# Attention's head on one core: the first unit's transfers split twelve to four between two queues, in place of eight to eight

## The chip, the cores and the metric

The kernel runs on one core of a Trainium2 chip. The time is the device time of one execution in microseconds. Before the change the median of three runs is 663.71 us (662.4 to 664.31).

## The reference

The input x is 4096 tokens of 128 numbers. Three blocks change it in turn, each with a residual:

```python
x = x + 0.5 * ffn(layernorm(x))      # 8 experts, top 2, hidden 176, and a shared expert
x = x + attn(layernorm(x))           # over 4096 fixed memory keys and values, one head of 128
x = x + 0.5 * ffn(layernorm(x))      # the same weights as the first
```

The attention is `softmax((x Wq + bq) K^T / sqrt(128)) V`, then `Wo` and `bo`. Only its output is kept; the update of the memory is not computed.

## The kernel before

The tokens are 8 groups of 512. The first block handles a group at a time (`ffn(0)`), then the attention, then the second block (`ffn(1)`). Each engine has a program of its own written out by hand, and semaphores are the only ties between them. An instruction stands behind all that is before it on its engine.

**The attention is cut in 16 units.** A unit is one group of 512 queries (four tiles of 128) against one half of the keys, 2048 of them. A unit has 8 steps, `h` = 0 to 7: two for each tile `i`, one for each 1024 of the keys. In a step:

- TensorE makes the scores of 128 queries by 1024 keys: six matmuls of 512 columns (`scores`, lines 1311 to 1313), in one of three pairs of PSUM banks. A pair is taken again once the exponential that reads it is done.
- VectorE takes the maximum (line 1061), and after a tile's second one the negative maximum (line 1067).
- ScalarE takes the exponentials (`exponentials`, lines 726 and 736).

For the product with the values the exponentials have to be transposed. There are two ways. Of **moved** tiles (tiles 0 and 1 in the first unit, 0 to 2 in the later ones) VectorE transposes squares of 32 by 32 (`transpose_squares`, line 1056), and DMA transfers put the strips in place (`move_strip`, line 331). Of the **own** tiles (2 and 3 in the first unit) TensorE transposes blocks of 128 into the bank `TB` (`transpose_pair`, line 1331).

**Rings.** The transposed exponentials of a unit are used in eight pieces, the rings. ScalarE rounds each into `p_hi`, with `moved_high` (line 708) for the moved tiles and `own_high` (line 700) for the own ones. GpSimd subtracts for `p_lo` of the moved (`moved_low`, line 513), VectorE for that of the own (`own_low`, line 1049). TensorE multiplies with the values (`values`, lines 1352 to 1354). There is only one bank `TB`, so `transpose_pair` of a ring waits until `own_low` of the ring before is done (line 1323). The order of ScalarE's program around the head is:

1. unit 0, step 5: the sixth exponential; then the waits of lines 789 to 791, then the transfers of lines 792 to 794;
2. step 6: the seventh exponential, then `moved_high` of ring 0, which first waits for all 256 counts of the semaphore `moved[0]`: sixteen transfers of 16;
3. step 7: `own_high` of ring 0, the eighth exponential, `moved_high` of ring 1.

TensorE's program has, at the first step of unit 1, scores, and the transposes of ring 0, which wait for the seventh exponential. At the second step it has scores, and the transposes of ring 1. The third has scores (they wait for the eighth exponential), the values of ring 0, the transposes of ring 2.

VectorE's program has `own_low` of ring 0 ahead of the maximum of the second step of unit 1. From there on every step of TensorE is one group of transposes, six matmuls of scores and six of values.

**The transfers of the first unit.** The two moved tiles are cut in 4 strips of 32 partitions (`i`), and each strip in 4 by the block `b` of queries within the tile: sixteen transfers of 128 KB. They can go once VectorE's four transposes of squares are done. SP issues those with `b` = 0 and 1 (lines 382 to 384), ScalarE those with `b` = 2 and 3. In the later units SP issues sixteen of 128 KB and twelve of 64 KB, and ScalarE four of 64 KB.

SP's program has nothing between the first unit's transfers and those of the second. They wait for squares of the second unit.

Of the kernel before, what the change touches and what calls it, by code (L numbers as in the profile page):

```python
# [45 lines left out]
QUADS = P // SQ  # L46
# [41 lines left out]
def macaron_kernel(nc: bass.Bass, x, wup, wdown, gate_w, expert_bias, shared_up, shared_down,  # L88
                   wq, bq, wo, bo, keys_values, out):
    with ExitStack() as ctx:  # L90
# [170 lines left out]
        def wait(eng, s, n):  # L261

            if not isinstance(n, int) or n > 0:
                eng.wait_ge(s, n)
# [21 lines left out]
        def early_logits(i):  # L286

            return (TB, banks[:, 3, :], banks[:, 1, :])[i][:, 0:GT * E]

        def moved_tiles(w):  # L290

            return 2 if w in (0, LAST) else MOVED
# [27 lines left out]
        def squares_of(units):  # L320
            return 2 * sum(moved_tiles(w) for w in range(units))
# [4 lines left out]
        def move_strip(eng, u, k, b, i):  # L326

            first, count = BATCHES[k]
            target = probsT[b * SQ:(b + 1) * SQ, u % 2, :, :, :].rearrange(
                "p (t i) c q -> p i t (c q)", t=MOVED)[:, i, first:first + count, :]  # L330
            eng.dma_start(target, E2[i * SQ:(i + 1) * SQ, first:first + count, b, :]).then_inc(moved[k], 16)
# [7 lines left out]
        def pair_at(H):  # L339

            return pairs_until(H) if pairs_until(H + 1) > pairs_until(H) else None

        def projection_at(H):

            w = H // HALVES - 2
            if w < 0 or w >= LAST:
                return None
            return w if H % HALVES == (FIRST_LAG if w == 0 else LAG) + 1 else None

        def tiles_of(g):  # L350
            return bass.ds(g * GT, GT)

        @block.sync
        def _(sp):
            sp.dma_start(X[:, 0:GT, :], x[:, 0:GT, :]).then_inc(x_loaded[0], 16)
            sp.dma_start(wup_f, wup).then_inc(up_w_loaded, 16)
            sp.dma_start(X[:, GT:2 * GT, :], x[:, GT:2 * GT, :]).then_inc(x_loaded[1], 16)
            small = [(sup_s[:, :, :], shared_up), (sdown_s[:, :, :], shared_down), (wq_s[:, :], wq), (bq_s[:, :], bq)]
            for dst, src in small:
                sp.dma_start(dst, src).then_inc(small_w_loaded, 16)  # L360
            sp.dma_start(X[:, 2 * GT:3 * GT, :], x[:, 2 * GT:3 * GT, :]).then_inc(x_loaded[2], 16)
            sp.dma_start(wdown_f, wdown).then_inc(down_w_loaded, 16)
            sp.dma_start(X[:, AHEAD * GT:, :], x[:, AHEAD * GT:, :]).then_inc(x_loaded[AHEAD], 16)
            for b in range(2):
                sp.dma_start(kv_stage[:, b, :], keys_values[:, b, :]).then_inc(kv_loaded[b % 2], 16)
            for dst, src in [(wo_s[:, :], wo), (bo_s[:, :], bo.to_broadcast([P, D]))]:
                sp.dma_start(dst, src).then_inc(out_w_loaded, 16)
            for b in range(2, KV):
                sp.wait_ge(kv_lo_done, b - 1)
                sp.dma_start(kv_stage[:, b % 2, :], keys_values[:, b, :]).then_inc(kv_loaded[b % 2], 16)  # L370

            for u in range(UNITS):
                if u == 0:
                    sp.wait_ge(z_done, GROUPS)
                    sp.wait_ge(down_done, GROUPS * SLOTS)
                wait(sp, moved_lo_done, UP * (u - 1))
                for k, (first, count) in enumerate(BATCHES):
                    if first >= moved_tiles(u):
                        continue
                    sp.wait_ge(squares_done, squares_of(u) + 2 * (first + count))  # L380

                    for b in range(QUADS // 2 if u == 0 else QUADS - k):
                        for i in range(QUADS):
                            move_strip(sp, u, k, b, i)
            for g in range(GROUPS):
                sp.wait_ge(x_updated, GROUPS + g + 1)
                sp.dma_start(out[:, tiles_of(g), :], X[:, tiles_of(g), :]).then_inc(stored, 16)
            sp.wait_ge(stored, 16 * GROUPS)
# [179 lines left out]
        def _(act):  # L568
# [25 lines left out]
            def exp_logits(G, logits):  # L594

                act.wait_ge(logits_done, G + 1)
                if G >= 2:
                    act.wait_ge(route_step, STEPS * route_event(G - 2) + 1)
                act.activation(expz[:, G % 2, :, :].rearrange("p t e -> p (t e)"), logits, ACT.Exp, scale=-1.0
                               ).then_inc(expz_done, 1)  # L600
# [16 lines left out]
            def copy_wbc(G, bank):  # L617
                act.wait_ge(wbc_done, G + 1)
                wait(act, weighted, (G - 1) * SLOTS)
                act.activation(wbc[:, G % 2, :], bank, ACT.Copy).then_inc(wbc_copied, 1)  # L620
# [66 lines left out]
            def early_copy(i, bank):  # L687

                if i == 0:
                    act.wait_ge(q_projected, GROUPS)  # L690
                else:
                    act.wait_ge(probsT_done, UP * LAST)
                act.wait_ge(xT_done, SECOND_LN + i + 1)
                act.activation(xT[i], bank, ACT.Copy).then_inc(xT_copied, 1)
# [46 lines left out]
            def copy_oT(w):  # L741

                act.wait_ge(pv_done, (w + 1) * KC)
                wait(act, out_proj_done, w)
                act.activation(oT[:, :], OB, ACT.Copy).then_inc(oT_copied, 1)
# [17 lines left out]
            for u in range(UNITS + 2):  # L763
                g = u // 2
                prepares = u % 2 == 1 and u < LAST
                for h in range(HALVES):
                    H = u * HALVES + h
                    w = projection_at(H + 3)
                    if w is not None:
                        copy_oT(w)  # L770
                    if u == LAST + 2 and h == LAG - 2:
                        copy_oT(LAST)
                    if u == LAST + 1 and h == 3:
                        early_copy(1, banks[:, 1, :])
                    if u == LAST + 1 and h == 5:
                        exp_logits(GROUPS + 1, early_logits(1))
                        early_copy(2, banks[:, 0, :])
                    if u == LAST + 1 and h == 7:
                        exp_logits(GROUPS + 2, early_logits(2))
                    if u == LAST + 2 and h == 3:  # L780
                        copy_wbc(GROUPS, banks[:, 2, :])

                    ring = pair_at(H + 3)
                    if ring is not None:
                        own_high(ring)
                    if u < UNITS:
                        exponentials(u, h // 2, h % 2)
                    if u == 0 and h == 5:
                        act.wait_ge(z_done, GROUPS)
                        act.wait_ge(down_done, GROUPS * SLOTS)  # L790
                        act.wait_ge(squares_done, squares_of(1))
                        for b in range(QUADS // 2, QUADS):
                            for i in range(QUADS):
                                move_strip(act, 0, 0, b, i)
                    if 0 < u < LAST and h == HALVES - 1:
                        wait(act, moved_lo_done, UP * (u - 1))
                        act.wait_ge(squares_done, squares_of(u) + 2 * MOVED)
                        for i in range(QUADS):
                            move_strip(act, u, 1, QUADS - 1, i)
                    if prepares and h == Q_HALF - 2:  # L800
                        copy_xT_for_q(g + 1, TB)
                    if prepares and h == Q_HALF - 1:
                        q_high(g + 1, TB)
                    if u == LAST and h == Q_HALF - 2:
                        early_copy(0, TB)
                    if u == LAST and h == Q_HALF - 1:
                        exp_logits(GROUPS, early_logits(0))
                    ring = pair_at(H + 4)
                    if ring is not None:
                        moved_high(ring)  # L810
                    w = projection_at(H + 2)
                    if w is not None:
                        copy_y(w)
                    if 2 <= u and u % 2 == 0 and h == 1:
                        shift_exponentials(g - 1)
# [668 lines left out]
```

## Time and profile before

| what | value |
|---|---|
| median of three runs | 663.71 us |
| the profiled execution, its own time | 662.44 us |
| its span, first to last instruction | 660.8 us |
| around the span | 1.6 us |
| mean granted TensorE clock | 0.984 of full |
| VectorE busy | 524.5 us (79%) |
| ScalarE busy | 461.3 us (70%) |
| GpSimd busy | 390.0 us (59%) |

Times inside the kernel are counted from the start of the span. The attention's head lies from 113 us on, the first unit's transfers from 130.7. A busy time of TensorE includes the pipelined ends of matmuls, so neighbouring rows overlap. "PEclk" is the granted clock: 1.00 is 2.4 GHz and 0.50 is 1.2 GHz. In the chain of work that ended last an entry "ACTq" is time in which ScalarE's queue issues a transfer. The issue of transfers is not counted as busy.

### The profile page before, as it was taken

How to read it: one execution, taken by the hardware profiler on the slowest of the kernel's cores; microseconds unless marked ns; L12 is line 12 of the kernel's file. 1: busy time of each engine (PE TensorE's matmuls, PEld its weight loads, DVE VectorE, ACT ScalarE, POOL GpSimd, SP SyncE). 2: the span in 40 equal slices, each digit the busy share in tenths (PEclk: the TensorE clock that was granted, in tenths of full speed). 3: DMA queues.
4: the chain of work that ended last, by engine and by line, in shares of the span. 5: the costliest groups of instructions: out<-in, count | busy, mean ns of one | idle time of the engine just before them, and what ended most of it. 6: DMA issues, size and time to landing. Idle time of an engine off the chain costs nothing.

```text
span 660.8 us, 9207 instructions
## 1 busy us (share of the span) xinstructions
PE 614.2 (93%) x2800; PEld 429.1 (65%) x2800; DVE 524.5 (79%) x943; ACT 461.3 (70%) x765; POOL 390.0 (59%) x427
## 2 busy tenths in 40 slices
PE   3899999669899999999999999999999988999997
PEld 2555434447677877777778777777777867645442
DVE  4788877758978888887797897887898957698785
ACT  3567888446668767777776777777776774668886
POOL 3876970025366867767687587696677786524000
PEclk9799999979999999999999999999999998999999
DMA  8012020052573553744735627437355350000000
GB/s 301 1 33 65 32 64 0 2 126 65 128 160 87 137 132 76 172 95 101 160 84 141 135 64 176 107 93 163 90 131 116 84 121 1 0 18 17 32 33 32
DMA packets 35555, 59.06 MB, mean 89 GB/s; under 512 B 8539, under 2 KB 9139, under 8 KB 35379
## 3 DMA queue, kind: packets, MB, share of 16 engines
q1 hardware_dynamic: 31891, 53.75, 33.4%
q10 hardware_dynamic: 3616, 4.73, 2.8%
q8 instruction: 23, 0.38, 0.3%
q14 instruction: 25, 0.20, 0.1%
HBM read 8.12 MB, written 2.10 MB: 15 GB/s over the span
## 4 chain that ended last, share of the span: by engine, by line
PE 67%; DVE 18%; issue 5%; ACT 5%; SPq 1%; POOL 1%; ACTq 1%; DMA 1%; DVEq 0%; POOLq 0%
PE banks L1311 7%; PE banks L1352 7%; PE banks L1353 7%; PE banks L1354 7%; PE banks L1313 7%; PE banks L1312 7%; PE banks L1331 5%; DVE bank_max L1061 4%; DVE E L1056 4%; PE banks L1195 4%; PE banks L1186 3%; PE banks L1202 3%; PE banks L1149 3%; DVE probsT L958 3%; PE banks L1362 2%
## 5 line engine op out<-in xcount | busy, mean ns | idle before, releaser
L513 POOL TENSOR_TENSOR p_lo<-probsT,p_hi 128x768 fp32r<-128x768 f32 (+1 forms) x128 | 226.8, 1775 | 161.9 <-ACT p_hi L708 161.1
L1061 DVE TENSOR_REDUCE bank_max<-banks 128x1 f32<-128x1024 f32 x128 | 156.1, 1220 | 34.8 <-PE banks L1313 33.7
L708 ACT ACTIVATE p_hi<-probsT 128x768 fp32r<-128x768 f32 (+1 forms) x128 | 104.5, 816 | 28.0 <-PE banks L1354 24.0
L1311 PE MATMUL banks<-kv_lo,q_parts 128*128 128x512 f32 x256 | 112.0, 437 | 6.9 <-ACT E L726 4.4
L958 DVE SCALAR_TENSOR_TENSOR probsT<-banks,E 128x1024 bf16<-128x1024 f32 x80 | 95.5, 1218 | 28.7 <-PE banks L1186 28.1
L1056 DVE STREAM_TRANSPOSE E<-E 128x1024 f32<-128x1024 f32 x92 | 113.5, 1234 | 1.7 <-ACT E L726 1.7
L726 ACT ACTIVATE E<-banks,neg_max 128x1024 f32<-128x1024 f32 x92 | 102.3, 1113 | 8.5 <-DVE neg_max L1067 5.3
L1352 PE MATMUL banks<-p_hi,kv_lo 128*128 128x512 f32 x256 | 108.1, 422 | 0.0
L615 ACT ACTIVATE probsT<-probsT 128x1024 bf16<-128x1024 bf16 x96 | 91.8, 981 | 18.7 <-DVE probsT L958 15.5
L1353 PE MATMUL banks<-p_lo,kv_hi 128*128 128x512 f32 x256 | 102.8, 401 | 0.0
L1354 PE MATMUL banks<-p_hi,kv_hi 128*128 128x512 f32 x256 | 102.6, 401 | 0.0
L1313 PE MATMUL banks<-kv_hi,q_parts 128*128 128x512 f32 x256 | 101.6, 397 | 0.0
L1312 PE MATMUL banks<-kv_hi,q_parts 128*128 128x512 f32 x256 | 101.5, 397 | 0.0
L700 ACT ACTIVATE p_hi<-banks 128x256 fp32r<-128x256 f32 (+1 forms) x128 | 52.3, 408 | 63.1 <-PE banks L1331 62.9
L1049 DVE TENSOR_TENSOR p_lo<-banks,p_hi 128x256 fp32r<-128x256 f32 (+1 forms) x128 | 56.1, 438 | 43.1 <-ACT p_hi L700 42.6
L1331 PE MATMUL banks<-ident,probs 128*128 128x128 f32 x272 | 53.5, 280 | 10.7 <-ACT probs L736 6.6
L1311 PEld LDWEIGHTS banks<-kv_lo,q_parts 128*128 128x128 f32 x256 | 48.6, 190 | 15.3 <-ACT E L726 5.8
L1331 PEld LDWEIGHTS banks<-ident,probs 128*128 128x128 f32 x272 | 36.9, 143 | 32.9 <-ACT probs L736 7.0
L1354 PEld LDWEIGHTS banks<-p_hi,kv_hi 128*128 128x128 f32 x256 | 48.4, 189 | 12.4
L1352 PEld LDWEIGHTS banks<-p_hi,kv_lo 128*128 128x128 f32 x256 | 48.5, 190 | 11.8 <-issue 1.7
L1353 PEld LDWEIGHTS banks<-p_lo,kv_hi 128*128 128x128 f32 x256 | 48.5, 190 | 11.7 <-issue 1.7
L1186 PE MATMUL banks<-E,wup_b 128*128 128x512 bf16 x176 | 53.6, 392 | 2.4 <-DVE q_parts L1018 1.1
(118 smaller groups left out, 886.3 us busy)
## 6 DMA issues: line engine op xcount, KB each, us to landing
probsT<-E SPq DMA_DIRECT2D x248, 128.0 KB, 2.4
probsT<-E SPq DMA_DIRECT2D x168, 64.0 KB, 2.0
E<-in_keys_values SPq DMA_DIRECT2D x8, 512.0 KB, 3.5
probsT<-E ACTq DMA_DIRECT2D x56, 64.0 KB, 2.3
out<-X SPq DMA_DIRECT2D x8, 256.0 KB, 2.0
X<-in_x SPq DMA_DIRECT2D x1, 1280.0 KB, 8.9
probsT<-E ACTq DMA_DIRECT2D x8, 128.0 KB, 4.1
X<-in_x SPq DMA_DIRECT2D x3, 256.0 KB, 5.1
```

Source lines behind the costliest of these rows:

```text
L513: pool.tensor_tensor(moved_part(p_lo, ring), moved_pair(ring // UP, ring % UP), moved_part(p_hi, ring).bitcast(fp32), ALU.subtract).then_i ...
L708: act.activation(moved_part(p_hi, ring), moved_pair(ring // UP, ring % UP), ACT.Copy).then_inc(moved_hi_done, 1)
L958: dve.scalar_tensor_tensor(hidden[:, k, :, :], up_banks[PAIR_BANK[k]], 0.0, spread.unsqueeze(1).to_broadcast([P, 2, N]), ALU.max, ALU.mult ...
L1056: dve.transpose(half, half).then_inc(squares_done, 1)
L1061: dve.tensor_reduce(bank_max[:, i % 2, h:h + 1], score_pair(u, i, h).rearrange("p b n -> p (b n)"), AX.X, ALU.max).then_inc(bank_max_done, 1)
L1311: pe.matmul(bank, qh, kl, start=True, stop=False)
L1312: pe.matmul(bank, ql, kh, start=False, stop=False)
L1313: pe.matmul(bank, qh, kh, start=False, stop=True).then_inc(scores_done, 1)
L1331: last = pe.transpose(TB[:, at_column:at_column + P], own_exponentials(w, t)[:, c * P:(c + 1) * P], ident[:, :])
L1352: pe.matmul(OB, vl, hi, start=(c == 0), stop=False)
L1353: pe.matmul(OB, vh, lo, start=False, stop=False)
L1354: pe.matmul(OB, vh, hi, start=False, stop=(c == KC - 1)).then_inc(pv_done, 1)
```

## The change

```diff
@@ SP
-                    for b in range(QUADS // 2 if u == 0 else QUADS - k):
+                    for b in range(QUADS - 1 if u == 0 else QUADS - k):
                         for i in range(QUADS):
                             move_strip(sp, u, k, b, i)
@@ ScalarE
                         act.wait_ge(squares_done, squares_of(1))
-                        for b in range(QUADS // 2, QUADS):
-                            for i in range(QUADS):
-                                move_strip(act, 0, 0, b, i)
+                        for i in range(QUADS):
+                            move_strip(act, 0, 0, QUADS - 1, i)
```

`QUADS` is 4. In the first unit SP issues the strips of `b` = 0, 1 and 2, twelve transfers, and ScalarE those of `b` = 3, four. The sixteen transfers are the same, they count on the same semaphore, and no wait changes. The later units are as before.

## Rows read from the trace of the kernel before

**Rows 1.** The page: busy time by engine, and the chain's shares by engine

```profile
PE 614.2 (93%) x2800; PEld 429.1 (65%) x2800; DVE 524.5 (79%) x943; ACT 461.3 (70%) x765; POOL 390.0 (59%) x427
...
PE 67%; DVE 18%; issue 5%; ACT 5%; SPq 1%; POOL 1%; ACTq 1%; DMA 1%; DVEq 0%; POOLq 0%
```

**Rows 2.** The chain in order of time, 133 to 148: start us, us, what

```profile
133.46 1.00 ACTq L331
...
137.86 1.20 ACTq L331
...
139.16 1.21 ACT probs L736 x2
...
140.42 1.12 PE banks L1331 x4
...
141.97 0.43 PE banks L1312
...
144.10 0.87 PE banks L1331 x4
...
146.37 0.24 PE banks L1352
146.60 0.23 PE banks L1353
...
147.78 0.44 PE banks L1331 x4
```

**Rows 3.** Timeline of TensorE: start, us, line, what, count [idle before <-releaser]

```profile
140.42 1.12 PE L1331 MATMUL banks<-ident,probs 128*128 128x128 f32 x4 [6.60 <-ACT probs L736]
```

**Rows 4.** Timeline of ScalarE, the same columns

```profile
142.07 0.63 ACT L708 ACTIVATE p_hi<-probsT 128x512 fp32r<-128x512 f32 x1 [1.70 <-DMA probsT<-E]
```

**Rows 5.** Timelines of VectorE and of TensorE's weight loads, the same columns

```profile
143.21 0.69 DVE L1049 TENSOR_TENSOR p_lo<-banks,p_hi 128x512 fp32r<-128x512 f32 x1 [6.93 <-ACT p_hi L700]
144.14 1.22 DVE L1061 TENSOR_REDUCE bank_max<-banks 128x1 f32<-128x1024 f32 x1 [0.23 <-PE banks L1313]
...
143.96 0.72 PEld L1331 LDWEIGHTS banks<-ident,probs 128*128 128x128 f32 x4 [0.58 <-DVE p_lo L1049]
```

**Rows 6.** Stretches: us, busy by engine, then PEclk, DMA share, GB/s

```profile
133.80:137.90 4.10, 0.02 (x1) 0.00 (x0) 2.44 (x11) 0.00 (x0) 0.00 (x0) 1.00 0.96 240
137.90:140.40 2.50, 0.00 (x0) 0.00 (x0) 0.00 (x0) 1.21 (x2) 0.00 (x0) 0.50 0.89 242
140.40:144.70 4.30, 4.28 (x14) 3.32 (x15) 1.25 (x2) 2.63 (x5) 1.28 (x1) 0.50 0.15 39
144.70:173.60 28.90, 28.73 (x134) 21.99 (x132) 25.21 (x40) 18.76 (x34) 16.07 (x22) 1.00 0.41 94
123.90:126.00 2.10, 0.00 (x0) 0.00 (x0) 2.06 (x4) 1.22 (x3) 0.00 (x0) 1.00 0.00 0
548.90:550.80 1.90, 0.02 (x1) 0.02 (x1) 0.77 (x2) 1.89 (x5) 0.21 (x1) 1.00 0.00 0
550.80:554.20 3.40, 3.40 (x11) 2.82 (x12) 3.30 (x6) 0.89 (x2) 3.32 (x4) 0.52 0.00 0
```

**Rows 7.** The same view, for the transfers: two queues, and SP's alone

```profile
132.00:141.20 9.20, 2.60 (x13) 1.91 (x11) 3.75 (x12) 1.21 (x2) 0.00 (x0) 0.82 0.91 226
160.00:167.00 7.00, 6.85 (x32) 4.98 (x32) 5.95 (x8) 4.10 (x9) 2.54 (x2) 1.00 0.93 204
```

**Rows 8.** Line 331: duration ns min/median/max, first and last start; landing by queue

```profile
L331 SPq DMA_DIRECT2D probsT<-E x3: 588/672/738, 130.7 to 132.1; - x3
L331 SPq DMA_DIRECT2D probsT<-E x2: 1096/1198/1300, 132.8 to 134.2; - x2
...
DMA to landing us min/median/max: 3.2/4.1/4.3
...
L331 SPq DMA_DIRECT2D probsT<-E x11: 596/597/607, 160.0 to 166.4; - x11
...
DMA to landing us min/median/max: 2.4/2.4/2.5
```

## The prediction

> **What bounds the kernel now.** I read the page first, for which engine carries the span. TensorE is busy 93% of it and holds 67% of the chain that ended last; the queues of SP, ScalarE and VectorE hold a per cent or so each [rows 1]. So TensorE sets the pace nearly everywhere, and the head of attention is an exception of a few microseconds. Then the chain in order of time, for that exception: it runs through ScalarE's queue to the last of its eight transfers, 137.86 + 1.20, only then through the seventh exponential (139.16), and from there to TensorE's four transposes at 140.42 [rows 2]. TensorE's own timeline shows the hole: it sits idle 6.60 us, from 133.8 to 140.42, until ScalarE's exponential releases it [rows 3]. The change is aimed at that wait.
>
> Third, ScalarE's timeline, for what stands behind the exponential in its program: at 142.07 the conversion of the first moved piece (line 708), after 1.70 us of waiting for the transfers to land [rows 4]. Behind it in the program is the conversion of the own piece (line 700). On VectorE the subtraction of that own piece starts at 143.21, after 6.93 us idle that line 700 ends, with the next maximum behind it at 144.14; and TensorE's weights for the second four transposes waited 0.58 us for it, to 143.96 [rows 5]. This is the second door. TensorE's own stream reached those transposes at 144.10 by the chain [rows 2], so the two doors opened within 0.14 us of each other. From 144.7 to 173.6 TensorE is busy 28.73 of 28.90 us [rows 6]: what comes late at 144 stays late.
>
> **The change, part by part.** Four transfers leave ScalarE's queue. It is a removal of the four last issues there: the fourth of eight begins at 133.46 and takes 1.00, the eighth ends at 139.06 [rows 2]. ScalarE is then free at 134.46 instead of 139.06, 4.60 us earlier. The seventh exponential moves with it, from 139.16 to 134.56, and the first four transposes from 140.42 to 135.82.
>
> What does TensorE then do? The transposes and the one score pair behind them (six matmuls), which took 140.42 to 144.10 at the low clock. At the full one they cost 0.44 + 6 x 0.235 = 1.85 us, by the transposes at 147.78 and 0.23 or 0.24 for a matmul [rows 2]. So they are over at about 137.7. Next are the second transposes (line 1331, ring 1), which overwrite the bank that VectorE must first have subtracted from (own_low of ring 0). That waits for own_high of ring 0, which stands on ScalarE behind moved_high of ring 0, which waits for all sixteen transfers. No other work of TensorE is ahead of this wait. VectorE's next maximum is queued behind the same subtraction, and GpSimd's subtraction of the moved piece waits for moved_high too. Everything gained up to 137.7 is therefore held until the landing plus 143.96 - 142.07 = 1.89 us [rows 4, 5].
>
> Four transfers join SP's queue. SP has nothing else to do until unit 1, so no instruction but the transfers themselves is delayed there. But do the last of them land at 142.07 as now? Two bounds. By bytes: sixteen transfers (2.1 MB) flowed from 132.0 to 141.2 at 226 GB/s with two queues; SP alone, in unit 1, moves 204 GB/s [rows 7]. ScalarE's last transfer would land near 133.46 + 4.1 = 137.6 [rows 2, 8], its data some 0.9 before (as 141.2 stands before 142.07). To 136.7 the rate stays 226: 1.06 MB. The other 1.04 MB at 204 take 5.1 us, so the data end at 141.8, 0.6 later than now. By issues: SP's third begins at 132.1, its fourth at 132.8, its fifth at 134.2, and that one still takes 1.1 us as it does beside the other queue; the seven after it go at the pace that SP has alone, 11 between 160.0 and 166.4, or 0.64 apart [rows 8]. The twelfth begins at 135.3 + 6 x 0.64 = 139.1 and lands 2.4 us (alone) to 4.1 us (in the crowd) later, 141.5 to 143.2. The ends are -0.6 and +1.1; I take +0.4, inside both and near the one by bytes, because the engines were 96% busy in this stretch and bytes bind first [rows 6].
>
> A page has a rule here. The Trainium skill (DMA: Bandwidth & Descriptors, section Issuing engines are not separate DMA queues) says that starting transfers from several engines saves the sequencer's time only, since all run on the same engines. By it the landing would stay at 142.07 and the sum below would be 0.4 us smaller. The 226 against 204 GB/s of the rows say otherwise, and the sum goes by the rows.
>
> Now the clock. Now it is granted in full until 137.9, 4.1 us after TensorE stopped, is half (1.2 instead of 2.4 GHz) from there, and comes back at 144.7, after 4.3 us of unbroken work [rows 6]. After the change TensorE works at about 135.8 to 137.7 at the full clock: a hole of 2.1 us (123.9 to 126) left the clock at 1.00 [rows 6]. Then it stands from 137.7 to about 144.35 (143.96 + 0.4), 6.6 us, as long as the present hole. So the clock falls again, in time to be low at 144.35. Now only the second transposes are cold behind the second door: 0.87 instead of 0.44, a loss of 0.43 [rows 2]. How long would it be low after the change? After 140.42 it took 4.3 us of work, after the other such return, at 550.8, about 3.4 [rows 6]. Between those two I take 3.8, from 144.35 to 148.15. The transposes lose 0.43; the other 2.93 us hold matmuls of 0.43 instead of 0.235, so they lose 2.93 x (1 - 0.235/0.43) = 1.33. Together 1.76.
>
> **The sum.** Start at the second door +0.25 (144.35 against 144.10); cold work behind it +1.76; cold work there today -0.43: +1.58, say +1.6 us. The 4.60 us that ScalarE wins are worth nothing, since they end in the wait for the landing. With the ends of the terms: landing -0.6 puts the start at 143.36, so -0.74, landing +1.1 gives +0.96; cold 3.4 us gives 0.43 + 2.53 x 0.453 = 1.58, cold 4.3 gives 1.98. From -0.74 + 1.58 - 0.43 = +0.4 to +0.96 + 1.98 - 0.43 = +2.5. The profiled execution took 662.44 us, span 660.8 and 1.6 around it, 1.27 under the median of the runs, 663.71; it would be 664.0, and a median 665.3.
>
> A measurement of this kernel can tell about 0.3% (2.0 us) from no change, so the forecast is slower, but under that line.
>
> **The rivals.** *The clock stays up.* The burst at 135.8 to 137.7 breaks the long hole in two. If that keeps the full grant until 144.35, the 1.76 is gone: +0.25 - 0.43, so -0.2, median 663.5, not slower. It is decided at one place: the granted clock when the second transposes start. For it: the hole of 2.1 us at 123.9 left the clock full. Against: the second hole is as long as the present one, in which the clock fell, and even the 1.9 us at 548.9 were followed by the low clock [rows 6]. Chance 13%. The Trainium skill (TensorE: Matmul & The Clock Gate, section HAM oscillation) says that each long idle gap makes the next burst start cold again; the trace agrees at 137.9.
>
> *A later landing.* SP's issues stay at 1.1 us for longer, or the clock needs over 4.3 us: the first is seen beside ScalarE's queue only, the second not after a hole of this kind. A landing at +1.1 makes the sum 0.96 + 1.76 - 0.43 = +2.3, 2 us more of cold at 0.453 each makes it +2.5: about +2.4, median 666.1. Chance 22%.
>
> *ScalarE's time goes through.* If the landing did not gate, TensorE would be 4.6 us early for good, 659.1. That needs 2.1 MB landed by 137.5, over 380 GB/s. Against it are the 226 GB/s and the 1.70 us wait in line 708 [rows 4, 7]. Chance 3%.
>
> *Nothing at all*: the loss is taken up later, where VectorE or the transfers of unit 2 set the chain for some microseconds: 663.7. VectorE's own waits for TensorE there speak against it, as all start from TensorE's late work. Chance 7%.
>
> **The numbers.** The forecast has 55%: 665.3, its own range from 664.1 to 666.2. The line at 665.7 cuts a quarter off its upper side (0.15), and most of the later landing lies above it (0.18): slower by over 0.3%, 0.33. Faster by over 0.3% is the third rival and a little of the first: 0.05. The rest, 0.62, is within. The range must hold the clock that stays up (663.5) and the later landing: 663.0 to 666.5, which leaves out the third rival and the tails.
>
> **What would show it.** In the new profile the seventh exponential starts near 134.6 and TensorE's hole of 6.60 is two: about 2 us before the first transposes and over 6 before the second, the latter ended by VectorE's line 1049. Line 708 waits over 6 us for the landing, at 142 to 143. The granted clock is 0.5 until about 148 instead of 144.7, and transposes, scores and values behind 144 take their long durations. SP's queue shows twelve issues, the last seven nearly 0.64 apart. The prediction is wrong if line 708 starts before 141.4, if the clock is full at 144.4, or if TensorE is not busy without a break from there to 173 + 1.6.

## The result, and the profile after

| | median of 20 runs | lowest to highest |
|---|---|---|
| before | 663.57 us | 660.48 to 665.49 |
| twelve and four | 665.47 us | 663.27 to 667.92 |

The ratio is 1.0043, with a 95% interval of 1.0031 to 1.0055: 0.43% slower (by the two medians alone it is 0.29%). A second series of the same kernel later gave 1.0023 (1.0009 to 1.0037). By the means of both series (32 runs, 665.37 +- 0.22) against 135 runs of the kernel before in five series (663.28 +- 0.12) it is 2.1 +- 0.25 us slower. The signs +- are standard errors here and below.

From the page of the changed kernel, the parts that answer to [rows 1]:

```profile
span 664.9 us, 9207 instructions
...
PE 615.2 (93%) x2800; PEld 429.4 (65%) x2800; DVE 525.9 (79%) x943; ACT 461.1 (69%) x765; POOL 390.4 (59%) x427
...
PE 62%; DVE 19%; issue 5%; ACT 5%; SPq 4%; DMA 2%; POOL 2%; DVEq 0%; ACTq 0%; POOLq 0%
```

No engine works noticeably more than before. ScalarE's queue has left the chain, and SP's has taken its place. The chain in order of time, which answers to [rows 2] (start us, us, what):

```profile
139.53 2.77 DMA probsT<-E
142.32 0.63 ACT p_hi L708
142.95 0.49 ACT p_hi L700
143.47 0.70 DVE p_lo L1048
144.22 1.12 PE banks L1330 x4
145.34 0.43 PE banks L1310
...
149.26 0.44 PE banks L1330 x4
```

TensorE's lines are one lower here, since the changed loop is a line shorter. SP's last transfer lands, lines 708, 700 and 1048 follow, and only then come the second transposes. Next the timelines of TensorE and of ScalarE [rows 3, 4]:

```profile
135.51 0.66 PE L1330 MATMUL banks<-ident,probs 128*128 128x128 f32 x4 [1.96 <-ACT probs L736]
...
144.22 1.12 PE L1330 MATMUL banks<-ident,probs 128*128 128x128 f32 x4 [6.64 <-DVE p_lo L1048]
```

```profile
134.25 1.11 ACT L736 ACTIVATE probs<-banks,neg_max 128x1024 f32<-128x1024 f32 x1 [2.78 <-DVE neg_max L1066]
...
142.32 0.63 ACT L708 ACTIVATE p_hi<-probsT 128x512 fp32r<-128x512 f32 x1 [6.86 <-DMA probsT<-E]
```

The hole of 6.60 us has become two, of 1.96 and 6.64 us, with two microseconds of work between them. The seventh exponential is early (3.84 us after ScalarE's first transfer instead of 8.44; the profile names VectorE's maximum before it, but that was done at 133.61, and ScalarE's fourth transfer was issued until 134.15), and line 708 now waits 6.86 us for the landing instead of 1.70. The clock, by stretches (the last three numbers are the granted clock, the DMA share and GB/s):

```profile
137.40:140.80 3.40, 0.18 (x1) 0.00 (x0) 0.00 (x0) 0.00 (x0) 0.00 (x0) 1.00 0.92 209
140.80:144.20 3.40, 0.00 (x0) 0.00 (x0) 0.73 (x2) 1.88 (x3) 1.17 (x1) 0.50 0.18 40
144.20:147.60 3.40, 3.38 (x10) 2.90 (x11) 1.94 (x3) 3.07 (x7) 1.38 (x2) 0.50 0.00 0
147.60:174.20 26.60, 26.42 (x124) 20.28 (x123) 23.57 (x37) 15.51 (x28) 13.95 (x19) 1.00 0.43 97
```

It fell to 1.2 GHz at 140.8, 3.4 us after TensorE had stopped for the second time. It stayed there for 3.4 us of work behind the second door, then TensorE was busy with no hole until near 174. Before, it was low there for 0.6 us only [rows 6]. SP's queue (line 331, duration ns min/median/max, first and last start), first all twelve, then from the sixth on:

```profile
L331 SPq DMA_DIRECT2D probsT<-E x12: 587/604/1295, 130.4 to 139.5; - x12
...
L331 SPq DMA_DIRECT2D probsT<-E x7: 596/603/1254, 135.0 to 139.5; - x7
```

**How much of it is the head.** I measure the head from ScalarE's first transfer to the copy of the first unit's output (line 745, which waits for TensorE). That is 172.35 - 130.72 = 41.63 us in the first profile of before, and 173.83 - 130.41 = 43.42 in this one: 1.8 us. The profiled executions differ by more, 4.1 us of span. The other 2.3 came elsewhere: about 0.4 near 174 and 0.65 near 198, where TensorE waits for ScalarE's exponentials and these wait for transfers, and 1.5 in a stretch of low clock at 202.3 to 205.7 that this execution had; against that, it had reached its first transfer 0.3 us earlier. The experiments had to tell whether these belong to the change.

### The profile page after: what moved, and what is told of

The parts are those of the page before. It is cut to its first block, busy times and chain, and to the rows that moved or that the text cites. A ratio compares the mean times of both kernels' runs of the same rounds, so it can differ in the third digit from the quotient of the medians.

```text
span 664.9 us, 9207 instructions
## 1 busy us (share of the span) xinstructions
PE 615.2 (93%) x2800; PEld 429.4 (65%) x2800; DVE 525.9 (79%) x943; ACT 461.1 (69%) x765; POOL 390.4 (59%) x427
## 4 chain that ended last, share of the span: by engine, by line
PE 62%; DVE 19%; issue 5%; ACT 5%; SPq 4%; DMA 2%; POOL 2%; DVEq 0%; ACTq 0%; POOLq 0%
PE banks L1310 7%; PE banks L1312 7%; PE banks L1311 7%; PE banks L1353 7%; PE banks L1351 7%; PE banks L1352 7%; SPq L331 4%; PE banks L1330 4%; DVE E L1055 4%; DVE bank_max L1060 4%; PE banks L1194 3%; DVE probsT L957 3%; PE banks L1185 3%; PE banks L1201 3%; PE banks L1148 3%
## 5 line engine op out<-in xcount | busy, mean ns | idle before, releaser
L1353 PEld LDWEIGHTS banks<-p_hi,kv_hi 128*128 128x128 f32 x256 | 48.4, 189 | 12.4
L1312 PEld LDWEIGHTS banks<-kv_hi,q_parts 128*128 128x128 f32 x256 | 48.7, 190 | 11.5
```

Source lines behind the costliest of these rows:

```text
L1312: pe.matmul(bank, qh, kh, start=False, stop=True).then_inc(scores_done, 1)
L1353: pe.matmul(OB, vh, hi, start=False, stop=(c == KC - 1)).then_inc(pv_done, 1)
```

## Experiments

All were timed beside the kernel before. The last column is the head as defined above, from each kernel's profile (with all sixteen on SP it is counted from SP's first transfer).

| kernel | mean us | before, same chip | difference | head us |
|---|---|---|---|---|
| before, first profile | | | | 41.63 |
| before again (again_8_8) | 663.16 | 662.78 | +0.4 +- 0.4 | 42.25 |
| twelve and four | 665.63 | 663.27 | +2.4 +- 0.4 | 43.42 |
| the same again (again_12_4) | 664.93 | 663.22 | +1.7 +- 0.4 | 43.36 |
| all sixteen on SP (sp16_act0) | 665.55 | 663.22 | +2.3 +- 0.4 | 44.34 |
| four on SP, twelve on ScalarE (sp4_act12) | 664.65 | 663.62 | +1.0 +- 0.7 | 42.33 |
| 12/4, filled (fill_12_4) | 665.27 | 663.22 | +2.1 +- 0.5 | 41.77 |
| 8/8, filled (fill_8_8) | 664.25 | 663.22 | +1.0 +- 0.3 | 41.28 |
| 8/8, narrow filling (tiny_8_8) | 664.36 | 663.62 | +0.7 +- 0.5 | 42.14 |
| 8/8, 56 narrow (tiny56_8_8) | 663.36 | 663.58 | -0.2 +- 0.6 | 42.15 |
| 8/8, other order (reorder_8_8) | 663.29 | 662.78 | +0.5 +- 0.4 | 42.12 |
| 12/4, other order (reorder_12_4) | 662.92 | 662.78 | +0.1 +- 0.4 | 42.35 |
| that, filled (reorder_fill_12_4) | 663.13 | 663.62 | -0.5 +- 0.7 | 40.17 |
| that, filled in 52 pieces (reorder_fill52_12_4) | 662.10 | 663.58 | -1.5 +- 0.6 | 40.19 |

**The two kernels once more.**

> The changed kernel once more, for a second profile. Theory (the landing holds everything, and the clock's return comes later): in the head line 708 starts 142 to 143, and the step from the second door to the next transposes takes about 1.8 us more than the 3.25 of a step at the full clock. The profile of the changed kernel was 4.1 us longer in its span than that of before, of which 1.8 arose in the head. If the rest (low clock again near 202, transfers of the third unit later by 0.65) was chance of that execution, this profile's shift behind 210 against before is 1.5 to 3 and the mean over the runs is 1.6 to 2.5 above before. The rival, that the change also costs something in the third unit every time, expects about 4 in this profile as well and a mean near 3.

> The kernel before once more, for a second profile and more times. Theory: its head is the same as in the first profile (line 708 at the first issue + 11.4 us, the step behind the second door 0.4 us longer than 3.25). The stretch from 170 to 212, which took 0.7 to 2.6 us longer in the four later profiles (eight and eight with filling among them) than in the first profile of before, takes longer here too, by about 0.7: then the first profile was a lucky one and this stretch is no effect of the split. The rival (the split, or the filling, costs there) expects it within 0.2 us of the first.

The head of twelve and four came out the same, 43.36. That of eight and eight was 0.6 longer than in the first profile: the low clock lasted until 145.4, 5.6 us of work instead of 4.3. So the head's loss is 1.8 us against the first profile and 1.1 to 1.2 against the second. Stretches and TensorE's timeline of the second profile of before:

```profile
139.80:145.40 5.60, 5.55 (x17) 4.33 (x18) 2.24 (x4) 3.53 (x7) 2.32 (x2) 0.50 0.12 30
```

```profile
143.45 1.12 PE L1331 MATMUL banks<-ident,probs 128*128 128x128 f32 x4
...
147.69 0.60 PE L1331 MATMUL banks<-ident,probs 128*128 128x128 f32 x4
```

The hole near 198 was 1.38 us in the first profile of before, 2.43 in the second, 2.03 in the changed kernel's first and 1.73 in its second. A low clock near 200 followed in the second profile of before too, and not in the second of the changed kernel. So the part of the 4.1 us that arose after 182 is chance of an execution: the first profile of before was a lucky one there. Over all fourteen profiles the low clock near 200 came in six, with both splits.

**Is it the landing, and not ScalarE's time?**

```diff
# sp16_act0
-                    for b in range(QUADS - 1 if u == 0 else QUADS - k):
+                    for b in range(QUADS - k):
...
-                        for i in range(QUADS):
-                            move_strip(act, 0, 0, QUADS - 1, i)
```

> All sixteen on SP, none on ScalarE: the same dose again. The seventh exponential waits for VectorE alone and starts near 134. Theory: it does not matter; the sixteenth issue starts at 130.7 + 15 x 0.64 = 140.3 and lands 2.4 later, line 708 at 142.7 to 143.2, so +0.4 to +0.9 over twelve and four: 2.0 to 2.8 us slower than before in the head. The rival (ScalarE's time counts, and twelve and four only gave half of it) expects it to be faster than twelve and four.

The sixteen issues on SP and ScalarE's line 708:

```profile
L331 SPq DMA_DIRECT2D probsT<-E x16: 587/597/736, 129.7 to 139.5; - x16
```

```profile
141.93 0.63 ACT L708 ACTIVATE p_hi<-probsT 128x512 fp32r<-128x512 f32 x1 [7.64 <-DMA probsT<-E]
```

ScalarE is wholly free, and the head is 0.9 us longer again. The landing comes 141.93 - 129.7 = 12.2 us after the first issue, against 11.9 with twelve and four (142.32 - 130.41) and 11.35 with eight and eight (142.07 - 130.72). More on SP, later landing, whatever ScalarE gains: the theory holds, the rival falls. But only 0.3 of the 0.9 us is the landing. The other 0.6 is the clock, which stayed low for 4.8 us of work behind the door in this execution, where it was 3.4 with twelve and four:

```profile
143.80:148.60 4.80, 4.78 (x14) 3.91 (x15) 3.01 (x4) 3.07 (x7) 2.72 (x4) 0.50 0.00 0
```

The mean shows nothing of these 0.9 us: +2.3 +- 0.4 here, +2.1 +- 0.25 with twelve and four.

```diff
# sp4_act12, against the kernel before
-                    for b in range(QUADS // 2 if u == 0 else QUADS - k):
+                    for b in range(1 if u == 0 else QUADS - k):
...
-                        for b in range(QUADS // 2, QUADS):
+                        for b in range(1, QUADS):
```

> The other direction: four on SP, twelve on ScalarE. Theory of two doors: now the first one is the late one. ScalarE's twelve take 3.7 us for four beside SP and then 0.64 each, to about 130.7 + 3.7 + 8 x 0.64 = 139.5 or, at the pace of the queue beside another, 143; the seventh exponential starts there, and line 708 follows it without a wait for the landing or with a short one. So between 0.5 and 4 us slower than before in the head, with the seventh exponential within 2 us of line 708. The rival (the landing alone counts) expects the same as twelve and four.

```profile
140.93 1.11 ACT L736 ACTIVATE probs<-banks,neg_max 128x1024 f32<-128x1024 f32 x1 [8.71 <-issue]
143.52 0.63 ACT L708 ACTIVATE p_hi<-probsT 128x512 fp32r<-128x512 f32 x1 [1.39 <-DMA probsT<-E]
```

Here the first door opens 9.78 us after the first issue (131.15) in place of 8.44, and TensorE's hole is 7.94 us. The second door is later too: the landing, line 708, comes 12.37 us after the first issue instead of 11.35. So TensorE's stream reaches the second transposes at 145.44, within 0.1 us of the door (143.52 + 1.89 = 145.41). The head is at the lower end of what was expected, only 0.1 to 0.7 longer than with eight and eight, and the mean is +1.0 +- 0.7. Of the four splits eight and eight lands first (11.35, against 11.9, 12.2 and 12.4), and its two doors open together. In the head either way from it loses.

**Is it the clock?** TensorE gets matmuls into its hole whose result nobody reads; the bank is written over later by the first values.

```diff
+            def fill(n):
+                for _ in range(n):
+                    pe.matmul(OB, kv_hi[:, 0, 0:P], q_hi[:, 0, :], start=True, stop=True)
...
                         scores(u, h // 2, h % 2)
+                    if H == 9:
+                        fill(24)
```

With eight and eight it is `H == 8` and `fill(26)`.

> Twelve and four, and 24 matmuls of 512 columns whose result nobody reads on TensorE behind the score pair of unit 1's second step: they take about 24 x 0.235 = 5.6 us of the 6.5 us hole. Theory: the clock stays full, the second door still opens at the landing + 1.9, and the 1.8 us of cold work behind it are gone: 0.0 to +0.5 us against before, faster than twelve and four by 1.5 to 2.2. The rival (the loss is only the later landing and SP's queue) expects no gain over twelve and four. If the added reads slow the transfers, line 708 is later than 142.4.

> Eight and eight, and 26 such matmuls behind the score pair of unit 1's first step (6.1 us of the 6.6 us hole). Theory: the clock stays full; the first transposes still start at 140.4, their step ends at 142.3, and the second door opens at 143.96 instead of 144.10, with 0.43 us less of cold work behind it: 0.5 to 0.6 us faster than before, no more. So with full clock in both, twelve and four and eight and eight lie within 0.5 us of each other. The rival (ScalarE's issue time is what TensorE waits for) expects that here the hole of 6.6 us still costs all of its 4.6, and that twelve and four with the filling is 4 us faster than this one.

Stretches, then TensorE's timeline, of the filled twelve and four:

```profile
144.00:147.40 3.40, 3.34 (x17) 2.74 (x18) 3.23 (x6) 3.08 (x7) 1.69 (x3) 1.00 0.00 0
```

```profile
144.06 0.66 PE L1330 MATMUL banks<-ident,probs 128*128 128x128 f32 x4 [0.91 <-DVE p_lo L1048]
...
147.37 0.60 PE L1330 MATMUL banks<-ident,probs 128*128 128x128 f32 x4
```

In the head both went as expected. The second door opens when it did, and the step behind it takes 3.31 us instead of 4.88 (144.22 to 149.10 in the changed kernel's timeline). The head of the changed kernel is 1.6 us shorter with the filling, and the two splits lie 41.77 - 41.28 = 0.5 apart. Unfilled they lie 43.39 - 42.04 = 1.35 apart by the means of the profiles, so about two thirds of the head's loss are the clock. But the whole time did not follow: 665.27 and 664.25, no gain in the one and a loss of 1.0 +- 0.3 in the other. That expectation was wrong, and what gave the gain back lay behind the head.

**What the filling cost.**

```diff
-                    pe.matmul(OB, kv_hi[:, 0, 0:P], q_hi[:, 0, :], start=True, stop=True)
+                    pe.matmul(OB[:, 0:SQ], kv_hi[:, 0, 0:P], q_hi[:, 0, 0:SQ], start=True, stop=True)
```

> Eight and eight with the same 26 added instructions in the same place, but 32 columns each in place of 512: they last 26 x 0.06 = 1.5 us at most and cannot fill the hole. The filling with 512 columns gained 0.4 us in the head and yet came out 1.0 +- 0.3 us slower than before. If the added instructions (code that has to be fetched, other places of the code) cost that time somewhere behind the head, this kernel is 1.0 to 1.5 us slower than before too. If the cost comes with the full clock or with the reads of the filling, it is within 0.4 us of before. The granted clock should fall in the hole as before.

It cost +0.7 +- 0.5 here as well, with the clock falling as before and a head of ordinary length. In the profile SP's transfers of unit 1 show it, and TensorE's hole near 174:

```profile
L331 SPq DMA_DIRECT2D probsT<-E x17: 590/598/1897, 157.8 to 169.7; - x17
```

```profile
173.87 0.50 PE L1311 MATMUL banks<-kv_lo,q_parts 128*128 128x512 f32 x1 [1.71 <-ACT E L726]
```

One issue among the first sixteen took 1.90 us instead of 0.60. A later exponential of ScalarE (line 726) waits for those sixteen. At that moment the trace has a fetch of code, one packet of 16 KB on queue q8. The DMA view, window 159 to 162:

```profile
q8 instruction: 1, 0.02, 3.1%
```

In the eight profiles without added instructions that fetch ran at 164 to 172, in four of them behind the sixteen and in four among them; in the four kernels with 36 to 52 added instructions it ran at 160 to 161. The next kernel (56 narrow matmuls in place of 26) tests whether the fetch moves with TensorE's program.

> Eight and eight with 56 of the narrow matmuls (6.2 us of the 6.6 us hole) in place of 26. In all four kernels with added instructions one fetch of 16 KB of code on queue q8 ran at 160 to 161 and one of SP's first six transfers of unit 1 took 1.3 to 1.9 us in place of 0.60; without added instructions the fetch ran at 164 to 172. If q8 carries TensorE's code (23 fetches of 16 KB, 5,934 TensorE instructions of 64 bytes are 0.38 MB), 60 more instructions put that fetch some 6 us earlier, ahead of SP's first transfer of unit 1 at 158: no issue among the first sixteen over 1.0 us, TensorE's hole near 174 back from 1.7 to about 0.5, and the mean 0.7 to 1.2 us under that of the kernel with 26. The rival (the added instructions cost something else) expects it as slow or slower than the kernel with 26.

Line 331 on SP, TensorE's timeline, and the DMA view of the window 155 to 158.2:

```profile
L331 SPq DMA_DIRECT2D probsT<-E x18: 585/598/606, 158.8 to 169.7; - x18
```

```profile
174.12 0.50 PE L1311 MATMUL banks<-kv_lo,q_parts 128*128 128x512 f32 x1 [0.38 <-ACT E L726]
```

```profile
q8 instruction: 1, 0.02, 2.4%
```

The fetch ran at 157.4, ahead of SP's first transfer; no issue was slow, and the hole is 0.38 instead of 1.71. So the profile shows the fetch as the cause of the slow issue and of the hole. The mean points the same way, but not beyond its noise: against before it is -0.2 +- 0.6 with 56 and +0.7 +- 0.5 with 26, 1.0 +- 0.8 apart.

The fourteen profiles fall in two groups by this fetch. Where it ran beside one of SP's first sixteen transfers of unit 1, one issue took 1.3 to 1.9 us and TensorE's hole near 174 was 0.95 to 1.71 us (eight profiles). Where it ran behind or ahead of them, the hole was 0.38 to 0.50 (six). That is the cost of the narrow filling, but not all of the wide one's. In fill_8_8 the head gained 0.8 against the mean of eight and eight and the hole lost 0.6, yet the mean is +1.0 +- 0.3; in fill_12_4 they are -0.3 and +1.2, and the mean is +2.1 +- 0.5. Some 1.1 to 1.2 us are unexplained in each.

**Does the second door hold the gain?** ScalarE's order at the head, with both splits:

```diff
                     ring = pair_at(H + 4)
-                    if ring is not None:
+                    if ring == 1:
+                        moved_high(0)
+                    if ring:
                         moved_high(ring)
```

> Twelve and four, and on ScalarE the conversion of the first moved piece (line 708, which waits for the landing) goes behind the own piece's conversion (line 700) and the eighth exponential. The second door then opens without the landing. Theory: the seventh exponential at 134.3, line 700 near 136.4, the second transposes near 137.8, the eighth exponential before 138.5, the next score pair done near 139.7; then TensorE waits for the values' input, landing 142.3 + 0.63 + 1.28 = 144.2. Against before, whose values start at 146.4, that is 2.2 us earlier, less the cold work from 144.2: 12 matmuls or so cold, 1.5 us. So 0 to -1.5 us against before and 2 to 3 us faster than twelve and four. The rival (the landing was not what held the gain) expects no difference from twelve and four.

> Eight and eight with the same order on ScalarE. Theory: the first transposes still wait for the seventh exponential at 139.2, so TensorE's stream reaches the second ones at 144.10 cold as now, the door being open already; no difference within 0.3 us. So the order is worth nothing with eight and eight and 2 to 3 us with twelve and four. The rival (the order alone frees the time) expects a gain here too.

TensorE's timeline of twelve and four in this order:

```profile
132.88 0.66 PE L1332 MATMUL banks<-ident,probs 128*128 128x128 f32 x4 [1.99 <-ACT probs L736]
...
134.95 0.66 PE L1332 MATMUL banks<-ident,probs 128*128 128x128 f32 x4
...
141.76 0.77 PE L1353 MATMUL banks<-p_hi,kv_lo 128*128 128x512 f32 x1 [4.75 <-issue]
```

The second transposes come 2.07 us behind the first, not 8.7. The work that was held goes ahead, and TensorE stops only at the values, which need the landing for their own sake. The head is 1.0 us shorter than twelve and four, where I had expected 2 to 3. The mean, each against the kernel before on its own chip, is 1.6 to 2.2 lower (+0.1 against +1.7 and +2.4). With eight and eight the order changed nothing, 42.12 against 41.63 and 42.25. It is the interplay: ScalarE's 4.6 us can reach TensorE only once the landing does not stand in front of line 700. Against the kernel before it was no gain, in the head (42.35 against 42.04) or in the mean. I had expected 0 to -1.5. The values started 13.97 us after the first issue, 1.7 earlier than the 15.65 of before and not 2.2, and they ran cold for 4.6 us, which by the prediction's rate of 0.453 costs 2.1 and not 1.5.

**Together.**

> Twelve and four, the other order on ScalarE, and 18 matmuls of 512 columns (4.2 us) in the hole of 4.75 us ahead of the first values. Theory: no low clock in the head; the values start 1.7 us earlier than in before, counted from the first issue, and nothing cold follows, which cost before 0.4: 2.1 us faster than before in the head, 2.8 faster there than the same kernel without filling. In the whole time 1 to 2 us faster than before, as the filling gave back 1.4 us in the other two kernels that had it. The rival (clock no matter) expects no difference from the kernel without filling.

The head is 40.17, 1.9 us under the mean of four profiles of eight and eight (42.04: before twice, and the two with narrow matmuls), and 2.2 under the same kernel unfilled. The filled eight and eight with this order was not run, so how much of it the split itself gives is not shown. The mean gained only 0.5 +- 0.7: a slow issue of 1.61 us was among the sixteen of unit 1, as the fetch ran at 160.1. So the last kernel splits the filling into 52 smaller matmuls:

```diff
+            def fill(n, width):
+                for _ in range(n):
+                    pe.matmul(OB[:, 0:width], kv_hi[:, 0, 0:P], q_hi[:, 0, 0:width], start=True, stop=True)
...
+                    if H == 8:
+                        fill(16, P)
+                    if H == 10:
+                        fill(36, 2 * P)
```

> Twelve and four, the other order on ScalarE, and the filling in smaller pieces: 16 matmuls of 128 columns in the first hole, 36 of 256 in the hole ahead of the values. The clock stays full in the head as with 18 of 512, and the 68 more instructions put TensorE's fetch ahead of unit 1's transfers. Theory: the head stays 1.5 to 2.1 us faster than before, the hole near 174 is under 0.8, and the mean is 1 to 2 us below before: faster than both kernels. The rival, that code has no part in it, expects the 663.1 of the kernel with 18.

Its stretch of the head, and TensorE's timeline:

```profile
133.00:146.00 13.00, 12.21 (x83) 10.62 (x82) 7.01 (x18) 6.15 (x11) 3.05 (x3) 1.00 0.60 141
```

```profile
144.25 0.47 PE L1353 MATMUL banks<-p_hi,kv_lo 128*128 128x512 f32 x1 [0.53 <-issue]
```

Median 662.04, mean 662.10 against 663.58 on the same chip: ratio 0.9979 (0.9957 to 1.0000). It has the lowest mean of all, 1.5 +- 0.6 us under before and, by the differences against before, 3.6 under twelve and four, and its head is as short as the last one's. The fetch ran at 155.5, ahead of SP's first transfer, and the hole near 174 is 0.38 instead of 1.43. Its interval just touches no change, and the 1.0 +- 0.9 us to the kernel with 18 is not clear of noise.

## Why the prediction was right

I had said 665.3, range 663.0 to 666.5, with a loss just under what can be told from no change. Measured were 665.47 and 664.97, a loss of 2.1 +- 0.25. The mechanism held. That the median was met to 0.2 us is in part luck: the head lost less than the sum says, and something that the sum lacks made up for it. The line of 0.3% was not met cleanly: the first series is above it (0.43%), the second below (0.23%), and all runs together are on it (0.32%).

- **The 4.60 us of ScalarE end in the wait for the landing.** Right. The exponential started 3.84 us after the first issue, as worked out (134.56 - 130.72). The landing and the second door are in the new chain, and the order of ScalarE alone opens that door.
- **The landing.** Taken as +0.4. It came 11.91 us after the first issue instead of 11.35: +0.56, close to the bound by bytes (+0.6). The issues were later than worked out: SP's sixth still took 1.25 us, so the twelfth began 9.1 us after the first and not 8.4, and it landed 2.8 us later. That bytes bind first is not shown: SP alone issues 131 KB every 0.64 us, which is 205 GB/s, the very rate that the bound by bytes used. Sixteen on SP are later still.
- **The start behind the door.** Taken as +0.25. It was 144.22 - 130.41 = 13.81 against 144.10 - 130.72 = 13.38: +0.43.
- **The clock.** Taken as low for 3.8 us of work; it was 3.4 and 3.3 in the two profiles. The step behind the door took 5.04 us by the chain against 3.68 [rows 2], +1.36, where the prediction had 1.76 - 0.43 = 1.33. The rival of a clock that stays up fell at the place that was named: 0.50 at 144.2. One premise was luck of the trace: the hole of 2.1 us before 126 left the clock full there, but the same hole (2.20 us in each) was followed by the low clock 1.3 to 1.5 us after its end in both profiles of twelve and four, and from 125.0 in the second of before. In the first of twelve and four:

```profile
127.20:130.60 3.40, 3.00 (x8) 1.84 (x7) 3.37 (x5) 1.42 (x3) 0.00 (x0) 0.50 0.02 5
```

  The burst at 135.5 did run at the full clock, as forecast.
- **The sum.** +1.58 against +1.79 in the first pair of profiles. The term that was too simple is the cold work "there today": 0.43 was one execution's. In the second profile of before the step took 4.24 us instead of 3.66 (by the timelines), so the head's loss is 1.1 to 1.8.
- **What the sum lacked.** The whole time lost 2.1 +- 0.25, the head about 1.35 (43.39 against the mean 42.04). The remaining 0.7 or so is not settled. A candidate is the fetch of code. With the same code on TensorE it ran among SP's sixteen in one of two profiles of twelve and four (TensorE's hole near 174: 0.95 and 0.41 us), with the other order (1.33), with sixteen on SP (1.43) and with four on SP (1.41), but behind them in all three of eight and eight (0.50, 0.38 and 0.38). Four of five against none of three is suggestive and too few to say that the split moves the fetch, or SP's transfers, onto each other.

The rule on issuing engines (the Trainium skill, DMA: Bandwidth & Descriptors, section Issuing engines are not separate DMA queues) would have had the landing unchanged, read as the prediction read it. The runs show it 0.56 later with twelve on SP, and 0.9 with sixteen. They do not show the rule wrong. It grants the sequencer's time to start a transfer, and as SP alone starts 131 KB every 0.64 us, that time alone could set the 205 GB/s.

## What to carry to other kernels

Before time is taken from a queue, look for the second thing that the same work waits for: here it opened 0.14 us after the first, so only the first 0.14 us could be won. A burst pulled forward in front of an unchanged wait can make the next one start at the low clock, and so cost more than it wins (here 1.35 us of the head). Reorder what stands in front of that wait, or keep TensorE busy through it. And compare several profiles before reading a difference of 1 us out of two.

## What the runs showed of the hardware

- **Two queues moved more than one.** Sixteen transfers flowed at 226 GB/s with two queues; SP alone moved 204 in the second unit [rows 7] and 205 in the first (sp16_act0, 132 to 141). With both queues at work each issue took about 1.1 us instead of 0.60. Whether SP alone is held by its issues, 0.64 us apart, or by the DMA engines, 92 to 93% busy, is not separated.
- **Fetched code delays transfers.** One 16 KB packet on q8 made SP's issue of 128 KB beside it last 1.3 to 1.9 us instead of 0.60. The place moves with the number of instructions in TensorE's program: 52 more (26 matmuls and their weight loads) moved it from 170 to 160, 112 more to 157. TensorE's hole near 174 was 0.6 to 1.3 us longer for it. That the whole time moves by as much is not clear of noise.
- **The clock's return differs from run to run.** Behind holes of the same length (6.60 and 6.56 us) it took 4.3 and 5.6 us of unbroken work. Its fall differs too: 4.1 us after TensorE stopped in the first, 1.9 in the second (133.3, low from 135.2). Two traces of one kernel can differ by 0.6 us in the head for that alone.
